# Two-pass mixture-of-experts kernel on one core: another PSUM bank for the fifth tile's down projection, a conversion moved up in the first turn, no GpSimd drain at the end, and 48 unused small products left out

## The reference

```python
x = x + xattn(layernorm(x), itok, ctx, ctx, ctx)   # layer 1: 4 experts, one for each token
x = x + ffn(layernorm(x), ...)                     # layer 2: routed and shared experts

# layer 1: the expert follows from the token's id; Wg, Wu and Wd are all the same 512x512 matrix
y = (silu(h @ Wg[e].T) * (h @ Wu[e].T)) @ Wd[e].T

# layer 2
h = rmsnorm(h, norm_w)
scores = softmax(h @ gate_w.T)                     # 32 experts, the best 4 for each token
buf[e, pos] = h[tok]                               # at most 512 rows for an expert
act = silu(buf @ w13[e][:, :256]) * (buf @ w13[e][:, 256:])
routed[tok] += w[tok, e] * (act @ w2[e])
out = h_in + routed + silu(h @ shared_gate) * (h @ shared_up) @ shared_down
```

## Time and profile before

| what | value |
|---|---|
| median of 3 runs | 632.4 us (631.36 to 632.88) |
| the profiled execution | 630.22 us |
| its span, first to last instruction | 628.5 us |
| TensorE busy in the span | 588.0 us |
| VectorE, ScalarE, POOL busy | 434.1, 358.3, 383.2 us |
| mean granted TensorE clock | 0.990 of full speed |

### The profile page before, as it was taken

The page is one execution under the profiler, slowest core; times in us unless marked ns, Lnnn a source line. Parts: engine busy times, 40 slices in busy tenths (PEclk is TensorE's granted clock), DMA queues, the critical chain, the costliest instruction groups (busy, mean ns, idle before and its releaser), DMA issues.

```text
span 628.5 us, 14609 instructions
## 1 busy us (share of the span) xinstructions
PE 588.0 (94%) x3666; PEld 511.3 (81%) x3667; DVE 434.1 (69%) x1017; ACT 358.3 (57%) x603; POOL 383.2 (61%) x434
## 2 busy tenths in 40 slices
PE   2899999999999998799999999999999999999991
PEld 1778788888788786698899889889889998988980
DVE  6778888877889877666575665666667576656630
ACT  5456666656422133666766666666576765766641
POOL 5835777646839795656574646656556564755442
PEclk9999999999999999999999999999999999999996
DMA  7511323347933484979999999998999999998744
GB/s 292 198 35 62 115 101 116 105 183 242 287 70 47 52 240 95 244 217 246 251 242 263 226 251 252 234 283 209 282 226 234 274 231 258 243 251 249 146 61 58
DMA packets 57295, 120.52 MB, mean 192 GB/s; under 512 B 7344, under 2 KB 8496, under 8 KB 56752
## 3 DMA queue, kind: packets, MB, share of 16 engines
q0 software_dynamic: 22720, 55.06, 41.1%
q1 hardware_dynamic: 34544, 65.10, 31.4%
HBM read 88.42 MB, written 36.96 MB: 199 GB/s over the span
## 4 chain that ended last, share of the span: by engine, by line
PE 54%; DVE 6%; issue 5%; DMA 3%; ACT 2%; DVEq 2%; POOL 2%; ACTq 1%; POOLq 0%; SPq 0%
PE sps_gu L211 6%; PE sps_gu L213 6%; PE sps_gu L212 6%; PE sps_t L211 4%; PE sps_t L212 4%; PE sps_t L213 4%; PE sps_y L213 4%; PE sps_y L212 3%; PE sps_y L211 3%; PE sps_cols L1177 2%; PE sps_table L211 2%; PE sps_table L212 2%; PE sps_table L213 2%; PE sps_rank L1177 2%; DVE r_hot L1488 2%
## 5 line engine op out<-in xcount | busy, mean ns | idle before, releaser
L1461 DVE TENSOR_TENSOR wl<-raw,wh 128x1024 fp32r<-128x1024 f32 x96 | 117.1, 1220 | 23.1 <-issue 16.3
L1298 ACT ACTIVATE wh<-raw 128x1024 fp32r<-128x1024 f32 x96 | 101.4, 1057 | 0.0
L1037 POOL DMA_INDIRECT out<-r_oh,scatter x32 | 52.3, 1635 | 58.9 <-ACT spare_tiles L1362 36.5
L211 PE MATMUL sps_gu<-s_xth,wh 128*128 128x256 f32 (+1 forms) x256 | 75.8, 296 | 2.2 <-issue 2.1
L212 PE MATMUL sps_gu<-s_xtl,wh 128*128 128x256 f32 (+1 forms) x256 | 75.8, 296 | 0.0
L213 PE MATMUL sps_gu<-s_xth,wl 128*128 128x256 f32 (+1 forms) x256 | 75.8, 296 | 0.0
L1037 POOL DMA_INDIRECT out<-r_rank,scatter x16 | 25.9, 1619 | 58.3 <-ACT r_oh L1362 38.9
L1014 POOL DMA_INDIRECT spare_tiles<-hb_dram,gather x48 | 48.2, 1003 | 18.8 <-issue 14.3
L211 PEld LDWEIGHTS sps_gu<-s_xth,wh 128*128 128x128 f32 x256 | 48.5, 190 | 4.7 <-issue 2.7
L212 PEld LDWEIGHTS sps_gu<-s_xtl,wh 128*128 128x128 f32 x256 | 48.5, 190 | 1.2
L213 PEld LDWEIGHTS sps_gu<-s_xth,wl 128*128 128x128 f32 x256 | 48.6, 190 | 0.0
(11 more groups left out here) (400 smaller groups left out, 1802.2 us busy)
## 6 DMA issues: line engine op xcount, KB each, us to landing
raw<-in_experts_w SPq DMA_DIRECT2D x192, 256.0 KB
craw<-in_ctx_w SPq DMA_DIRECT2D x4, 1024.0 KB, 7.8
out<-hb_dram SPq DMA_DIRECT2D x4, 1024.0 KB, 12.9
out<-both POOLq DMA_DIRECT2D x13, 256.0 KB, 4.4
both<-hb_dram SPq DMA_DIRECT2D x10, 256.0 KB
spare_tiles<-hb_dram SPq DMA_DIRECT2D x6, 256.0 KB, 4.9
spare_tiles<-hb_dram,gather POOLq DMA_INDIRECT x48
sraw<-in_sg SPq DMA_DIRECT2D x1, 512.0 KB
```

Source lines behind the costliest of these rows:

```text
L211: pe.matmul(acc, left_hi, right_hi, start=start, stop=False)
L1037: pool.indirect_dma_start(m.out, bass.IndirectOffsetOnAxis(ap=sidx[0:n, j:j + 1], axis=0), e_y[j][0:n], None, compute_op=ALU.add).then_inc ...
L1298: nc.scalar.activation(m.wh[:, b, ROWS[part]], m.raw[:, b, ROWS[part]], ACT.Copy).then_inc(e_hi[b][part], 1)
L1461: dve.tensor_tensor(m.wl[:, b, ROWS[part]], m.raw[:, b, ROWS[part]], m.wh[:, b, ROWS[part]].bitcast(F32), ALU.subtract).then_inc(e_lo[b][p ...
```

## The change

The diff has four parts.

- The 48 unused products of pass 1 go.
- `down(4)` writes to `sps_y` instead of `sps_t0`. It waits for `gated(0, 1)` of the running turn, the last reader of `sps_y`; the last chunk of `gate_up(1)`, which writes `sps_y` next, waits for `scaled(4)`; and `down(0)` waits for `scaled(2)` of the turn before instead of `scaled(4)`.
- In the first turn alone `high_rows(4)` and `low_rows(4)` stand earlier: by two places on ScalarE, by three on VectorE.

```diff
-        m.block = top.enter_context(nc.Block())
+        m.block = top.enter_context(nc.Block(no_gpsimd_drain=True))
...
-        e_py = (ps_t[0], ps_t[1], ps_t[0], ps_t[1], ps_t[0])
+        e_py = (ps_t[0], ps_t[1], ps_t[0], ps_t[1], ps_y)
...
-                if q == RING // 2 - 1:
-                    keep_busy(pe, m, ps_gu[1], 2 * WARM)
...
                         pe.wait_ge(e["sil" if o < CI else "a"], 2 * (k - 1) + o % CI + 1)
+                        if b == 1 and e_gu[o] is ps_y:
+                            wait(pe, e["y"], 5 * turn)
...
-                wait(pe, e["y"], 5 * turn + (0, -1, 1, 2, 3)[j])
+                if j == 4:
+                    pe.wait_ge(e["a"], 4 * (turn + 1) + CI)
+                elif not isinstance(turn, int) or turn > 0 or j >= 2:
+                    wait(pe, e["y"], 5 * turn + (-2, -1, 1, 2)[j])
...
                 high_rows(2, turn)
                 high_rows(3, turn)
+                if first:
+                    high_rows(4, turn)
                 weights(0, "rows_c", turn)
                 high_a(0, 1, turn)
                 if not first:
                     columns = columns_of(act, m.tab2, 1, turn - 1)
                     scaled(2, columns[0], turn - 1)
-                high_rows(4, turn)
                 if not first:
+                    high_rows(4, turn)
...
                 low_rows(3, turn)
+                if first:
+                    low_rows(4, turn)
                 gated(0, 1, turn)
                 low_weights(0, "rows_c", turn)
                 low_half(0, 1, turn)
-                low_rows(4, turn)
+                if not first:
+                    low_rows(4, turn)
```

## The result

The changed kernel takes 621.82 us (median of 4 runs, 621.38 to 623.98), the kernel before 632.01 us (4 runs, 631.36 to 632.88). The ratio is 0.9845, 95% interval 0.9818 to 0.9872: faster by 10.2 us, where 10.6 was forecast. The profiled execution takes 621.42 us with a span of 619.7, so it is 8.8 us shorter than that of before; time minus span stays at 1.7. Of the executions of the kernel before that stand beside the experiments one, on the fourth chip, was slow (982.76 us at a mean granted clock of 0.564); it is in no ratio, and without it the median there would be 0.1 us lower.

A forecast was written before the change was run, and what follows sets the result against it. TensorE, busy 588.0 of 628.5 us, was taken as the bound, so only its idle time and the end count. Savings of 4.8 + 1.0 + 4.8 + 0 = 10.6 us gave 632.4 - 10.6 = 621.8, range 619.0 to 627.0.

The forecast's parts named there:

- The sum: Whole kernel: savings of 4.8 + 1.0 + 4.8 + 0 = 10.6 us, giving a median of 621.8 us.
- the bank: Routed turns: moving down(4) to sps_y removes TensorE's 14 waits for scaled(2); worth 4.8 us, bounds 0 and 5.9.
- the first turn: Ahead of gate_up(1): tile 4's conversions moved earlier let TensorE go on 1.0 us sooner; bounds 0 and 2.1.
- the 2.2 us that I carried over: Whole kernel: the median of three runs was 2.2 us above the profiled execution; the forecast kept that difference.
- the 2 us under which the prediction called itself wrong: Routed turns: the forecast is wrong if TensorE gains under 2 us there.
- The drain: Kernel's end: GpSimd's drain of 4.85 us goes and the time stays saved; 4.8 us, bounds 0 and 4.85.
- it comes back behind the span: Kernel's end: GpSimd's drain time returns after the span; span falls 10.6, time 5.8, to 626.6 us; chance 0.20.
- the yardstick of 2.74 us: Routed turns: time of twelve unstalled 512-column matmuls, taken as what down(3) with down(4) need without a wait.
- The amount given back: Routed turns: low_rows(4) about 0.12 us late for gate_up(1) in about 8 long turns, returning 1.0 us.
- The next wait: Routed turns: low_rows(4) late by 0.3 us in all turns, losing 4.5 instead of 1.0; 625.3 us; chance 0.13.
- The clock in pass 1: Pass 1: without the unused products the clock falls for up to 5.7 us, costing 2.2 net; 624.0 us; chance 0.10.
- The slower rival: Routed turns: the gated product, with 1.0 us of room, holds up down(4); 2.0 us later gives 636.8; chance 0.03.

The follow-up runs named there:

- the first comparison: The changed kernel against the kernel before, on the chip where both were measured first: 621.82 us against 632.01, ratio 0.9845.
- the earlier trace: Profiled execution of the kernel before, nothing changed, from which the prediction was made: 630.2 us, span 628.5.

## Why the prediction was right, and where it wasn't

- **The sum.** Forecast 621.8, measured 621.82. That they agree so closely is luck. For the profiled execution the forecast was 619.6, and 621.42 was measured, 1.8 us more: 1.4 of it by the bank, 0.4 by the end of the program, 0.2 by pass 1, less 0.1 for the first turn. And the 2.2 us that I carried over from the profiled execution to the median are 0.4 in the changed kernel, 1.8 less. The two cancel. On the other chips the loop gained nothing by the bank, and all that TensorE gained in the turns was the first turn's 1.1 us and what the clock gives: about the 2 us under which the prediction called itself wrong.
- **The profile and the median.** The medians differ by 10.2 us, the profiled executions by 8.8. The 1.4 us between them are what a fall of the clock in the first turn costs, which the profiled execution of before doesn't have. That its other runs on the first chip had this fall is an inference from the other three chips; more late products in them would do as well.
- **The drain**: forecast 4.8. From the end of TensorE's last matmul to the end of the span the first comparison has 14.0 us before and 9.6 after, 4.4 less. Over all traces it is 13.9 to 14.3 us in the seven with the one drain and 9.3 to 9.6 in the five without, 4.8 less in the mean. Time minus span is unchanged, in two kernels. The rival "it comes back behind the span" (0.20) is out. The rule of the Trainium skill that I had weighed ("VectorE: DVE Perf Modes", section "The DRAIN you can't avoid") led to the right side, but its 12 ns is for the runtime's own drains and doesn't describe the one at the end of GpSimd's program, 4,852 ns here.
- **The bank**: the mis-sized term, "Their mean, 0.42, lies half way between 0.18 and 0.63" and so 5.9 us. The step that failed is the yardstick of 2.74 us from the earlier trace rows: behind the transposes the pair takes 2.87 us without any stall (the first matmul of `down(3)` is followed by the second after 0.33 us, the others after 0.23), so a wait cost 0.05 or 0.50. With seven turns of each kind that is 3.85 us, and all of them cost 3.89 (311.99 against 308.10). The amount given back was mis-sized the other way, 0.45 instead of 1.0, and it was lost in the three turns of 22.09 to 22.22 us. The "gap that is always there between two loads" is 0.04 in these rows, not 0.07; the 0.07 was part of the wrong yardstick. I could have seen it: the turn of the earlier trace rows took 2.92, and no turn took less than 2.88.
- **What made the stall.** The prediction took the two kinds of turn as given and never asked why there are two. The long kind comes from 1.4 us of VectorE's time upstream. Made on purpose, that delay gives the stall of the earlier trace rows with the old bank and none with the new one, so the chain from `gated(1, 1)` through `gated(0, 1)` and ScalarE's `scaled(2)` to `down(4)` is shown. The delay isn't the program's alone: the trace of the same program on the fourth chip has none, nor have those of other kernels on the second and third chip without the added line. But it isn't the first chip's alone either, since one turn with more drains on the fourth chip had it. Why VectorE starts late is open. One rival can be read from the traces. In the first one a gather of GpSimd starts 0.2 us ahead of the time at which the product is due in eight of the nine late turns, and 0.1 to 0.2 us behind it in the five turns of the loop that are on time. But on the fourth chip one starts 0.3 us ahead in 13 turns, none of them late. So its place alone doesn't do it.
- **The next wait** (0.13): `low_rows(4)` is indeed what comes last now, at 0.14 us for 14 turns with every product 1.5 us late. The sentence "some 0.1 us late" was right in kind, its 1.0 us too much.
- **The first turn**: forecast 1.0, 1.1 by the wait. The step that failed is the one on the clock: I had judged from the earlier trace rows that 1.9 us without a matmul keep the clock up. In four of the seven traces with that idle time (2.1 us ahead of `gate_up(1)`) the clock fell behind it, and by the mean clock it did in two of three runs of the kernel before. By the rule of the Trainium skill ("TensorE: Matmul & The Clock Gate", section "What's actually happening") idle time gives the clock back to its throttled state. That agrees with these runs, and I had counted the first turn against it on one execution.
- **The clock in pass 1** (0.10): it fell in the profiled execution and by inference in most runs without the products, so the rival had the mechanism right. The price was 1.3 us at 155 us, not 2.85; the wait for tiles covered 0.7 of it, and later waits all but 0.2.
- **The slower rival** (0.03) wasn't met and wasn't tested either. With the product of the large block 1.5 us late, `gated(0, 1)` starts 0.2 to 0.3 us behind tile 4's transposes, and in the trace it stood 0.2 behind them already (351.61 against 351.40). The 1.8 us were counted from there. Without a late product it starts 0.9 us ahead of them, so the room is larger by 1.1 us on the other chips.

No kernel tried here beats the changed one by more than can be told.

## What to carry to other kernels

Take the yardstick for a stall from the same place in a turn that doesn't stall, not from the same instructions elsewhere. Where turns come in two kinds, look upstream for what sets the kind before pricing the stall: it may be absent on the next chip, and a bank that decouples it is then worth nothing. And look at the block's end and at every idle time of TensorE of two microseconds: the first may hold a GpSimd drain that nobody needs, the second may cost about as much in clock as can be saved of the wait.

## What the runs showed of the hardware

- GpSimd's drain at the end of a program with software DMA: 4,852 ns in each of the seven traces that have it alone, 2,795 with earlier drains, 46 behind another one. Without it neither span nor time pays.
- Behind the same 2.1 us of idle time TensorE's granted clock was 1.00 in one execution and 0.50 from 265.8 to 269.1 us in another of the same program. In pass 1, behind 2.4 us, it fell in one execution of the changed kernel and not in the next. With 1.0 us of idle time in the first turn it fell there in none of the traces.
- The same program has turns of 22.0 and 22.5 us mixed in one trace and of 22.01 us throughout in one on another chip. The difference is VectorE starting a gated product 1.4 us late; the cause isn't known.
